# A four-layer graph attention kernel: attention scores as extra columns of the projections, their rows turned once per stage; 1300 instead of 1408 columns in the first layer's second chunk

## What is computed

```
# layer 0: 8 heads of 64
feats = x @ kernels[h];  a_s = feats @ attn_self[h];  a_n = feats @ attn_neigh[h]
p = exp(-(a_s[:, None] - a_n[None, :])**2) * (adj > 0);  p = p / (p.sum(1) + EPS)
out_h = p @ feats + biases[h]
# layer 1
out = adj @ (x @ W) + b
# layer 2
e = leaky((x@W1)@a_w [:, None] + (x@W2)@a_w [None, :] + a_b);  e = where(adj > 0, e, -9e15)
out = softmax(e, 1) @ (x @ fc_w + fc_b)
# layer 3: 4 heads of 128, Xh = the head's 128 columns of x
Xw = Xh @ W[h];  f1 = Xw @ V[h,0];  f2 = Xw @ V[h,1];  sig = sigmoid(f1[:, None] + f2[None, :])
# masked softmax of adj*sig, attention, batch norms, two MLPs, attention again
```

## Time and profile before

| | us |
|---|---|
| median of 3 runs (3787.44 to 3789.86) | 3789.41 |
| the profiled execution, own time | 3787.66 |
| its span, first to last instruction | 3786.1 |
| PE busy (share of the span) | 3400.1 (90%) |
| DVE busy | 2330.3 (62%) |
| ACT busy | 1679.4 (44%) |
| POOL busy | 271.1 (7%) |

### The profile page before, as it was taken

The page is one execution under the profiler, slowest core; times in us unless marked ns, Lnnn a source line. Parts: engine busy times, 40 slices in busy tenths (PEclk is TensorE's granted clock), DMA queues, the critical chain, the costliest instruction groups (busy, mean ns, idle before and its releaser), DMA issues. The chain is left out here.

```text
span 3786.1 us, 39785 instructions
## 1 busy us (share of the span) xinstructions
PE 3400.1 (90%) x13931; PEld 2134.0 (56%) x13931; DVE 2330.3 (62%) x2850; ACT 1679.4 (44%) x1527; POOL 271.1 (7%) x459
## 2 busy tenths in 40 slices
PE   7899999999978899995999995999999967999995
PEld 4433333333323677773555553877777735888884
DVE  4488888988966455555555553777777734122226
ACT  1288888888852111112222223777777702000002
POOL 1000000000002011110000001000010000000003
PEclk9999999999999999997999997999999989999997
DMA  7500000000012455553222224666666630866653
GB/s 284 179 16 8 15 8 15 16 8 15 8 44 91 189 222 229 218 215 137 79 87 94 94 79 175 233 243 244 244 243 245 231 141 15 369 272 269 273 219 123
DMA packets 109759, 557.51 MB, mean 147 GB/s; under 512 B 14320, under 2 KB 20432, under 8 KB 85584
## 3 DMA queue, kind: packets, MB, share of 16 engines
q1 hardware_dynamic: 88592, 432.35, 30.7%
q0 software_dynamic: 21056, 123.65, 8.5%
HBM read 363.77 MB, written 192.18 MB: 147 GB/s over the span
## 5 line engine op out<-in xcount | busy, mean ns | idle before, releaser
L528 PE MATMUL bank<-dist,hf 128*65 128x512 f32 (+1 forms) x2112 | 860.7, 561 | 63.3 <-ACT dist L491 63.3
L528 PEld LDWEIGHTS bank<-dist,hf 128*65 128x65 f32 x2112 | 277.4, 138 | 637.7 <-issue 489.3
L1354 PE MATMUL bank<-pt,HA 128*128 128x256 f32 x1936 | 505.1, 381 | 3.0 <-DMA HA<-features 3.0
L491 ACT ACTIVATE dist<-dist 128x1408 f32<-128x1408 f32 x352 | 469.2, 1368 | 1.5
L1543 PE MATMUL bank<-w,EM 128*128 128x256 f32 x1936 | 427.0, 381 | 12.7 <-DMA w<-weights 12.7
L993 PE MATMUL bank<-HB,pt 128*128 128x512 f32 x968 | 436.7, 593 | 0.0
L1543 PEld LDWEIGHTS bank<-w,EM 128*128 128x128 f32 x1936 | 369.7, 191 | 63.6 <-DMA w<-weights 12.9
L422 DVE TENSOR_TENSOR dist<-msk,sB 128x1408 f32<-128x1408 uint8 x208 | 337.0, 1620 | 74.7 <-PE bank L528 68.5
L1342 PE MATMUL bank<-idt,v 128*128 128x128 f32 x1936 | 304.4, 278 | 79.5 <-ACT pt L1232 50.7
L482 ACT ACTIVATE dist<-dist,neg_t 128x1408 f32<-128x1408 f32 x208 | 305.2, 1467 | 151.9 <-DVE dist L422 151.9
L1354 PEld LDWEIGHTS bank<-pt,HA 128*128 128x128 f32 x1936 | 328.6, 191 | 26.8 <-DMA HA<-features 3.4
(11 more groups left out here) (161 smaller groups left out, 3684.9 us busy)
## 6 DMA issues: line engine op xcount, KB each, us to landing
w<-weights SPq DMA_DIRECT2D x44, 2816.0 KB, 9.9
weights<-pt SPq DMA_DIRECT2D x220, 512.0 KB, 3.8
al<-in_adj_cols SPq DMA_DIRECT2D x22, 1408.0 KB, 7.5
at<-in_adj_tiles SPq DMA_DIRECT2D x22, 1408.0 KB, 6.7
rows<-in_adj_rows SPq DMA_DIRECT2D x22, 1408.0 KB, 6.8
mrow<-in_adj_rows POOLq DMA_DIRECT2D x22, 1354.0 KB, 8.3
rows_low<-mrow POOLq DMA_DIRECT2D x22, 1354.0 KB, 5.1
rows<-rows_low POOLq DMA_DIRECT2D x22, 1354.0 KB, 8.5
```

The costliest lines, as they stand in the source:

```text
L491: act.activation(d[:, :], d[:, :], ACT.Exp, scale=-1.0).then_inc(p_ready, 1)
L528: mm = pe.matmul(sums_bank(hh, k)[0:FW, 0:(b - a) * P], hf[hh][:, m, :], d[:, a * P:b * P], start=(m == 0), stop=(m == T - 1))
L1354: t = pe.matmul(acc_t[n % 2][:, 0:P2], HA[:, m, h * D3:(h + 1) * D3], pt[n % 2][:, m, :, :].rearrange("p r n -> p (r n)"), start=(m == 0), ...
```

## The change

Score vectors become columns of the weights. In stage P the weights are `w0x`, two halves of 256 + 8 columns: each half of the projection is a product of 264 columns into a bank of its own (`pj`, `sc`), the neighbour scores behind the first 256 columns and the self scores behind the second. In stage M the halves are 258 and 256 columns, in stage S four blocks of 128 + 2. The score products and ACT's score copies are gone; DVE copies all out of the two banks, four operations a tile where there was one. Scores that are needed as rows are kept as columns (`scol`, `f2`, `f3`) and turned once at the end of the stage (`turn_rows` on PE, `keep_rows` on ACT), then stored by POOL: two stores at the end of stage P, one at the end of M and of S. Weights are loaded in halves or blocks, so in pieces of 1 KB (stages P, M) and 512 B (S) a partition instead of 8 and 2 KB. In stage G the second chunk has VALID = 1300 columns instead of 1408, on all engines.

```diff
-        def project(pe, n, xt, w, u_col, u_row, heads, blocked=False):
+        def project(pe, n, xt, w, cols):
             pe.wait_ge(turned_out, n + 1)
...
             wait(pe, proj_out, n)
-            for k in range(KT):
-                if blocked:
-                    t = pe.matmul(pj[0:P, k * D3:(k + 1) * D3], xt[:, k, :], w[:, k, :], start=True, stop=True)
-                else:
-                    t = pe.matmul(pj[0:P, :], xt[:, k, :], w[:, k, :], start=(k == 0), stop=(k == KT - 1))
+            at = 0
+            for half, width in zip((pj, sc), cols):
+                for k in range(KT):
+                    t = pe.matmul(half[0:P, 0:width], xt[:, k, :], w[:, k, at:at + width],
+                                  start=(k == 0), stop=(k == KT - 1))
+                at += width
             t.then_inc(proj_mm, 1)
+        def turn_rows(pe, cols, width, released):
+            pe.wait_ge(*released)
+            pe.transpose(etp[0:width, 0:128], cols, idt[:, :]).then_inc(rows_turned, 1)
+        def keep_rows(act, n, width, rows_sb):
+            act.wait_ge(rows_turned, n)
+            act.activation(rows_sb[0:width, :], etp[0:width, 0:128], ACT.Copy).then_inc(rows_out, 1)
@@ stage P
-                    sp.dma_start(w0_sb[:, :, :], w0).then_inc(w_in, 16)
+                    for b in (0, 1):
+                        sp.dma_start(w0x[:, :, b, 0:D // 2], w0[:, :, b * (D // 2):(b + 1) * (D // 2)]).then_inc(w_in, 16)
...
                     def feats_out(n):
                         dve.wait_ge(proj_mm, n + 1)
-                        dve.tensor_copy(HA[0:P, n, :].rearrange("p (h w) -> p h w", w=FW)[:, :, 0:F0],
-                                        pj[0:P, :].rearrange("p (h f) -> p h f", f=F0)).then_inc(proj_out, 1)
+                        into = HA[0:P, n, :].rearrange("p (h w) -> p h w", w=FW)
+                        dve.tensor_copy(into[:, 0:H0 // 2, 0:F0], pj[0:P, 0:D // 2].rearrange("p (h f) -> p h f", f=F0))\
+                            .then_inc(part_out, 1)
+                        dve.tensor_scalar(neg_t[0:P, n, :], pj[0:P, D // 2:D // 2 + H0], -1.0, None, ALU.mult)\
+                            .then_inc(part_out, 1)
+                        dve.tensor_copy(scol[:, :, n], sc[0:P, D // 2:D // 2 + H0]).then_inc(part_out, 1)
+                        dve.tensor_copy(into[:, H0 // 2:H0, 0:F0], sc[0:P, 0:D // 2].rearrange("p (h f) -> p h f", f=F0))\
+                            .then_inc(proj_out, 1)
@@ stage G, DVE, ACT and PE alike
-                                        dve.tensor_tensor(d[:, :], msk[:, m, c * CW:(c + 1) * CW], sB[hh][:, :],
+                                        dve.tensor_tensor(d[:, 0:VALID[c]], msk[:, m, c * CW:c * CW + VALID[c]], sB[hh][:, 0:VALID[c]],
@@ stage M
-                    sp.dma_start(w_sb[:, :, :], fc_w).then_inc(c_in, 16)
+                    sp.dma_start(w_sb[:, :, 0:D // 2], fc_w[:, :, 0:D // 2]).then_inc(c_in, 16)
+                    sp.dma_start(w_sb[:, :, D // 2 + 2:D + 2], fc_w[:, :, D // 2:D]).then_inc(c_in, 16)
```

216 lines of the change are left out of this document (97 added, 119 removed).

## The result

| | before | after |
|---|---|---|
| median of 4 runs | 3788.43 us (3785.74 to 3789.86) | 3704.62 us (3702.85 to 3707.18) |
| profiled execution, its span | 3787.66, 3786.1 | 3702.97, 3701.1 |

The ratio is 0.9781, 95% interval 0.9768 to 0.9795: 84 us less. The forecast was 3695 us with a range of 3668 to 3736. The time is 9.6 us above it and well inside the range. One of its four terms, stage M, was wrong by more than half, and the experiments are mainly about that one.

What follows compares the result with a forecast made beforehand. PE was taken as the bound nearly everywhere, with second loops close behind. Stages P -9, G -30, M -27 and S -27 sum to -93 us, so 3787.7 becomes 3695 us, range 3668 to 3736.

Steps and rivals of the forecast that it cites:

- What bounds the kernel, and the first look at what comes second: Whole kernel: PE is the bound nearly everywhere; what comes second in P, M and S decides how much saving is kept.
- PE's part: Score products gone (1.86 us), projection 0.17 us longer: PE saves 1.69 us a tile in M, 1.85 in S.
- P, the period: Stage P: PE waits for DVE's four copies; period 5.1 us against 5.83, 20 tiles x 0.7 = -14 us.
- P, the start: Start of stage P: loading the weights in 1 KB pieces costs +1 us, bounds nothing to 2.5 us.
- G: Stage G, second chunk 108 columns narrower: 3.7 us for each of 8 groups, -30 us, bounds 25 and 34.
- M: Stage M: tile 21.2 to 19.7 us, the `mrow` loop as long as the tile now; -27 us, bounds -35 and -8.
- S: Stage S: loop through the load of `rows` and the exponential bounds; mean tile 23.85 us, -27 us, bounds -40 and -16.
- The sum: Whole kernel: -9 - 30 - 27 - 27 = -93 us, giving 3695 us, 0.975 of the time before.
- (A): Rival, chance 0.22: second loops in M and S give way to PE's saving; -114 us, 3673 us.
- (B): Rival, chance 0.16: second loops in M and S hold in full, P gains nothing; -44 us, 3744 us.
- (C): Rival, chance 0.02: waits drop PE's clock to 1.2 GHz in P and a tenth of M and S; 3860 us.
- (D): Rival, chance 0.02: half-bank passes do not hide weight loads, P and M lose 1.3 us a tile; 3795 us.

## Why the prediction was right, point by point

- **What bounds the kernel, and the first look at what comes second**: right in where to look, in part wrong in what is found there. P is held by DVE's copies, though the loads stand only 0.3 us a tile behind them, M by the `mrow` loop, S by the way to the exponential, but not by the link in it that the forecast named.
- **PE's part**: the projection was to grow by 0.17 us. The prediction's own rows give 0.06 (3.6 - 3.54) for 264 columns and less for 258; it measured 0.14 in M. The 0.2 us that the regular pass behind the score products also cost was not seen, so PE's saving in M is 1.9 us a tile and not 1.69; the changed kernel kept less than half of it.
- **P, the period**: forecast 5.1 us, measured 4.96 (copies at 105.59 and 110.55; 4.99 in the mean of 20); the four operations of DVE take 0.91 us from the first start to the last end, against 0.92 forecast. From the second projection to the last copy -16.3 us, forecast -14.
- **P, the start**: mis-sized. Four times the price: +4.3 us against +1. The bounds went to 2.5, so the measured value lay outside them. The step read the landing of the weights themselves (6.0 us against 4.9) and not that of the small loads issued behind them, for which DVE waits. The end of the stage was +3.3, forecast +4.4. That the stage came out at -8.6 for -9 is luck: the three misses, -2.3, +3.3 and -1.1 us, cancel.
- **G**: right, -31.2 for -30, and 29.6 by the run without it.
- **M**: the mechanism is right and the size wrong: -11.5 for -27, and as little as -2 in other executions. The step that failed is the tile at 19.7 us. Over 21 tiles the stage gained 17.5 us where the forecast had 30, a mean tile of 20.4 us: one took 28.7, the others 19.3 to 20.6. The forecast saw that the store would come to overlap with the tile load and put no price on it; the way from store to load went from 6.03 to 6.65 us, and to 11.6 once, where the store came just behind that load. The lag at the end was put at +1.5 and is 4.7 (22.5 us from the last tile to the next stage, 17.8 before). PE's own floor was put at 19.5 us and is 19.3. The earlier trace rows alone give the loop 20.9 us with the landing of 8.3, 18.6 with the best of 6.0, on either side of that floor; the landing that came, 7.0, makes it 14.88 - 1.3 + 6.03 = 19.6, and the store's growth the rest. The bounds (-35 and -8) held the profiled -11.5, but not every execution.
- **S**: -28.8 for -27. The regular period is 23.57 us and the mean of 19 tiles 23.87, for a forecast mean of 23.85. The size is right and two steps are not. The forecast's loop ran over the load of `rows`; with that load issued early the regular period stayed at 23.57, and it fell to 22.63 only when the maximum was taken ahead of the copy of group 4. And the split: ACT's order was to bring 1.04 us and brought 0.46 (25.04 to 24.58), since PE's own work is 24.58 us with the products. Without them it is 22.63, not 23.2, and of these 1.95 us the changed kernel kept 0.7 in the mean. That the mean of two loops came out so near is partly luck.
- **The sum**: 84 us for 93. M gave 15 less than forecast, and without layer 3's scatter nothing else is off by more than 2.
- **Rivals.** (A) did not come by itself, but its place was right: with `mrow` in halves M gives more than the 34 us that A took for it, 40. M came out between the forecast and (B) in the profiled execution, beyond (B) in others; P and S did not go (B)'s way. (C) came in one tile only: behind the wait of 7.27 us the clock fell, for 2.4 us. The waits of about 1 us in each tile of P and S cost no clock: it is 1.00 in P from 60 to 150 us and in S from 1780 to 2180. (D) did not come: sixteen narrow passes take 3.28 us where eight wide ones took 3.14.

## What to carry to other kernels

When work is taken from the engine that bounds a stage, add up the next loop from its parts (issue, landing, the other engine's work, landing) and not only from its period, which equals the tile's as long as it has slack; the new tile is no shorter than the larger of the two sums. The landings in that sum are those of the old timing. As the tile shrinks the transfers move against each other, so ask which one a store will fall beside: in M that was worth up to 5 us in one round. A single buffer that is loaded, changed and stored is such a loop, and going round it in halves took all of it away at no cost in bytes (28.9 us). And a load in small pieces is paid by whoever waits for what is issued behind it.

## What the runs showed of the hardware

- A 1 MB load in 1 KB pieces beside 3 MB of another queue delayed VectorE's first operation by 4.3 to 5.3 us: the small load that it waits for was issued 1.3 to 1.7 us later and landed 2.7 to 3.9 us later after its issue. Issued behind the small loads, the pieces landed in 15.0 us; with the other queue quiet, in 7.1.
- The store of 1.35 MB to HBM landed in 5.1 us in the median before, in 6.0 where it came closer to the load of 1.4 MB on the other queue, and once, 0.55 us behind that load, only after 10.9 us. From such a store to the issue of the next load behind it it was 6.1 to 7.5 us where the store was issued 0.6 us or more ahead of the tile load, 9.2 to 11.6 where it was issued 0.4 us ahead to 0.6 behind, 10.5 to 10.9 at 0.8 to 1.2 us behind it and 6.2 to 6.4 at 5.4 behind. In halves of 0.68 MB it landed in 3.4.
- After one wait of 7.27 us in a stage otherwise at full clock, fp32r passes of 512 columns started 0.43 us apart for 5.6 us, then 0.23 again. Waits of about 1 us in every tile of 5 us (stage P) or 24 us (stage S) left the granted clock at 1.00.
- An fp32 projection in sixteen passes of 258 and 256 columns takes 3.28 us where the engine has regular fp32r passes before and behind, and eight of 512 take 3.14; the fp32r pass behind narrow score products and eight wide passes comes 0.21 us later to its successor than behind the sixteen. Why is not known.
